# A latent-attention stack on one core: the second stage issues the same calls in another order

## What is computed

```python
x = x + _L0_xattn_ref(_layernorm(x, axis=-1), ctx_512, ...)
x = x + _L0_attn_ref(_layernorm(x, axis=-1), ...)
x = x + _L0_ffn_ref(_layernorm(x, axis=-1), ...)
x = x + _L1_xattn_ref(_layernorm(x, axis=-1), ctx_512, ...)
x = x + _L1_attn_ref(_layernorm(x, axis=-1), ...)
x = x + _L1_ffn_ref(_layernorm(x, axis=-1), ...)
```

## Time and profile before

| | us |
|---|---|
| median of three runs (1688.26 to 1689.56) | 1689.56 |
| the profiled execution, its own time | 1687.6 |
| its span in the profile | 1685.8 |
| the stage, first `score_x` to last `keep_hT` | 199.2 to 541.2 |

### The profile page before, as it was taken

One profiled execution on the slowest core, in us unless ns is written; L12 is line 12 of the kernel. 1 busy time (PEld: TensorE's weight loads), 2 busy tenths in 40 slices (PEclk: granted clock), 3 DMA queues, 4 the chain that ended last, 5 costly groups with the idle time before them and its releaser, 6 DMA issues. The chain is left out here.

```text
span 1685.8 us, 34006 instructions
## 1 busy us (share of the span) xinstructions
PE 1557.3 (92%) x14224; PEld 1087.3 (64%) x14224; DVE 1128.5 (67%) x1745; ACT 595.8 (35%) x1038; POOL 553.1 (33%) x885
## 2 busy tenths in 40 slices
PE   7999679989996588999999999999999996999999
PEld 3444357867783356777777777777777774565556
DVE  4665487588564667888877888878888833644433
ACT  2223134335332344444544444444444431111110
POOL 1200052123111344664554664554654431000000
PEclk9999779999996889999999999999999997999999
DMA  7533300010000012211212211212211113200000
GB/s 214 158 92 93 69 1 1 14 38 2 1 1 0 23 27 48 55 45 34 55 33 55 54 43 35 48 41 55 48 49 37 41 28 116 116 1 0 13 1 13
DMA packets 150536, 75.76 MB, mean 45 GB/s; under 512 B 128304, under 2 KB 131632, under 8 KB 148592
## 3 DMA queue, kind: packets, MB, share of 16 engines
q1 hardware_dynamic: 150384, 73.60, 17.1%
HBM read 55.73 MB, written 17.83 MB: 44 GB/s over the span
## 5 line engine op out<-in xcount | busy, mean ns | idle before, releaser
L1719 DVE SCALAR_TENSOR_TENSOR acc<-PS,wc,acc 128x504 f32<-128x504 f32 (+2 forms) x384 | 281.4, 733 | 93.2 <-ACT acc L1452 84.1
L2004 PE MATMUL PS<-HT,wgu 128*128 128x512 f32 x384 | 173.9, 598 | 0.6 <-ACT HT L2050 0.6
L1452 ACT ACTIVATE acc<-PS,wc 128x512 f32<-128x512 f32 x128 | 87.7, 685 | 171.8 <-PE PS L1183 120.0
L1183 PE MATMUL PS<-HT,wv 128*128 128x512 f32 x256 | 128.6, 626 | 11.4 <-DVE acc L1719 11.4
L1183 PE MATMUL PS<-HT,wkq 128*128 128x512 f32 x256 | 124.4, 610 | 6.6 <-DVE acc L1719 4.7
L1729 DVE SCALAR_TENSOR_TENSOR y<-th,acc 128x512 f32<-128x512 f32 x128 | 114.6, 895 | 22.7 <-ACT th L1456 21.5
L1642 POOL TENSOR_TENSOR rr<-nm,con 128x16 f32<-128x16 f32 x16 | 46.8, 2925 | 239.3 <-DVE nm L1747 239.3
L1200 PE MATMUL PS<-wz,HT 128*128 128x256 f32 x512 | 123.5, 389 | 0.8 <-DMA wz<-in_gdn_w 0.8
L2004 PEld LDWEIGHTS PS<-HT,wgu 128*128 128x128 f32 x384 | 73.3, 192 | 74.9 <-issue 72.8
L1346 PE MATMUL PS<-wo,ogT 128*128 128x256 f32 x512 | 115.3, 383 | 3.5 <-DVE dl L1782 2.4
L2140 DVE SCALAR_TENSOR_TENSOR act<-th,PS 128x512 f32<-128x512 f32 x48 | 33.0, 687 | 127.4 <-ACT th L2064 127.4
(11 more groups left out here) (252 smaller groups left out, 3045.6 us busy)
## 6 DMA issues: line engine op xcount, KB each, us to landing
a_rows<-AT SPq DMA_DIRECT2D x16, 512.0 KB, 2.6
wk<-in_l0x_k SPq DMA_DIRECT2D x16, 384.0 KB, 3.6
wgu<-in_moe_gu SPq DMA_DIRECT2D x6, 1024.0 KB, 14.9
queries_scratch<-tts SPq DMA_DIRECT2D x32, 128.0 KB, 2.7
wkq<-in_gdn_w SPq DMA_DIRECT2D x16, 256.0 KB, 2.7
wv<-in_gdn_w SPq DMA_DIRECT2D x16, 256.0 KB, 2.8
wz<-in_gdn_w SPq DMA_DIRECT2D x16, 256.0 KB, 3.3
wo<-in_gdn_w SPq DMA_DIRECT2D x16, 256.0 KB, 2.9
```

The source lines that it names most:

```text
L1183: mm = pe.matmul(PS[:, QB[q], :], w[:, o:o + DK], HT[:, k, f * 512:(f + 1) * 512], start=(k == 0), stop=(k == DC - 1))
L1452: a.activation(acc[:, f, :], PS[:, QB[q], :], ACT.Copy, scale=wc[:, h % 2, 4 * c + 3:4 * c + 4]).then_inc(s["tap"], 1)
L1719: v.scalar_tensor_tensor(a0, p0, wc[:, h % 2, 4 * c + 2 - k:4 * c + 3 - k], a0, ALU.mult, ALU.add).then_inc(s["conv"], 1)
L2004: mm = pe.matmul(PS[:, 2 * (i % 2) + w, :], wgu[:, m, k, w, :], HT[:, k, f * N:(f + 1) * N], start=(k == 0), stop=(k == DC - 1))
```

## The change

The lists of calls of all five engines in `phase2` are written in another order. No function, buffer, semaphore or wait changes, and each list has the same calls as before. SP loads tile 1 ahead of tile 0. Cut to the parts that the text speaks of:

```diff
-                load(0); load(1); load(2); load(3); load(4); load(5); load(6); load(7)
+                load(1); load(0); load(2); load(3); load(4); load(5); load(6); load(7)
...
-                score_x(0, 0); fold_down(); score_x(0, 1); score_x(1, 0); score_x(2, 0); turn_x(0, 0); score_x(3, 0)
-                turn_x(0, 1); context(0); score_x(1, 1); out_x(0); score_x(2, 1); turn_x(1, 0); turn_x(1, 1); turn(0, 0)
-                context(1); project(0, 0); out_x(1); turn_x(2, 0); scores(0, 0); turn_x(2, 1); score_x(3, 1); turn(1, 0)
...
-                down(7); turn(4, 3); turn_p(5, 1); scores(6, 1); values(5, 1); turn(7, 2); project_out(5, 1); project(7, 1)
-                turn(5, 3); turn_p(6, 1); scores(7, 1); values(6, 1); project_out(6, 1); turn(6, 3); turn_p(7, 1)
-                values(7, 1); project_out(7, 1); turn(7, 3)
+                score_x(1, 0); score_x(0, 0); fold_down(); score_x(0, 1); score_x(1, 1); score_x(2, 0); score_x(3, 0)
+                turn_x(0, 0); turn_x(0, 1); context(0); turn_x(1, 0); out_x(0); score_x(2, 1); turn_x(1, 1); score_x(3, 1)
+                context(1); turn_x(2, 0); out_x(1); turn(0, 0); turn_x(2, 1); project(0, 0); context(2); turn(1, 0)
+                turn_x(3, 0); scores(0, 0); project(1, 0); turn_x(3, 1); out_x(2); context(3); scores(1, 0); turn_p(0, 0)
...
+                down(6); project(5, 1); up_gate(7, 1); scores(5, 1); turn_p(4, 1); turn(6, 2); down(7); project(6, 1)
+                values(4, 1); turn(7, 2); project_out(4, 1); scores(6, 1); turn_p(5, 1); project(7, 1); values(5, 1)
+                turn(4, 3); scores(7, 1); project_out(5, 1); turn_p(6, 1); values(6, 1); project_out(6, 1); turn(5, 3)
+                turn_p(7, 1); turn(6, 3); values(7, 1); project_out(7, 1); turn(7, 3)
...
-                exp_x(0, 0); keep_fold(); exp_x(0, 1); keep_x(0, 0); keep_x(0, 1); exp_x(1, 0); keep_context(0); exp_x(2, 0)
-                exp_x(1, 1); keep_x(1, 0); exp_x(2, 1); keep_x(1, 1); keep_hT(0, 0); exp_x(3, 0); keep_context(1)
+                exp_x(1, 0); exp_x(0, 0); keep_fold(); exp_x(0, 1); keep_x(0, 0); keep_x(0, 1); exp_x(1, 1); keep_context(0)
+                keep_x(1, 0); exp_x(2, 0); exp_x(3, 0); keep_x(1, 1); exp_x(2, 1); keep_context(1); keep_x(2, 0)
...
-                share_x(0, 0); share_x(0, 1); scale_down(0); share_x(1, 0); scale_down(1); share_x(1, 1); root(0, 0)
+                share_x(1, 0); share_x(0, 0); share_x(0, 1); scale_down(0); share_x(1, 1); scale_down(1); share_x(2, 0)
...
-                spread_x(0, 0); sums_x(0, 0); spread_x(0, 1); butterfly(0); sums_x(0, 1); butterfly(1); spread_x(1, 0)
-                butterfly(2); sums_x(1, 0); spread_x(2, 0); spread_x(1, 1); residual(0, 0); spread_x(2, 1); sums_x(1, 1)
...
-                spread_x(4, 0); sums(2, 1); residual(1, 3); key_blocks(3, 1); stats(1, 3); spread_x(4, 1); apply(1, 3)
-                mask_spread(3, 1); sums_x(4, 0); residual(2, 3); sums(3, 1); stats(2, 3); sums_x(4, 1); spread_x(5, 0)
...
+                spread_x(1, 0); spread_x(0, 0); sums_x(1, 0); sums_x(0, 0); spread_x(0, 1); butterfly(0); sums_x(0, 1)
+                butterfly(1); spread_x(1, 1); butterfly(2); sums_x(1, 1); spread_x(2, 0); residual(0, 0); spread_x(3, 0)
...
+                apply(3, 2); residual(1, 3); stats(1, 3); spread_x(4, 0); apply(1, 3); key_blocks(3, 1); spread_x(4, 1)
+                mask_spread(3, 1); residual(2, 3); spread_x(5, 0); stats(2, 3); sums(3, 1); apply(2, 3); sums_x(4, 0)
...
+                mask_spread(6, 1); apply(4, 3); key_blocks(7, 1); sums(6, 1); mask_spread(7, 1); residual(5, 3)
```

More of the change, by code:

```diff
@@ L701, in _ @@
[L701 to L715, removed]
@@ new lines, in _ @@
+                turn_x(3, 0); scores(0, 0); project(1, 0); turn_x(3, 1); out_x(2); context(3); scores(1, 0); turn_p(0, 0)
+                turn(2, 0); out_x(3); values(0, 0); project(2, 0); project_out(0, 0); turn(3, 0); turn_p(1, 0); project(3, 0)
+                scores(2, 0); turn(0, 1); values(1, 0); hadamard(0); project_out(1, 0); up_gate(0, 0); scores(3, 0)
+                turn(1, 1); hadamard(1); turn_p(2, 0); up_gate(1, 0); values(2, 0); up_gate(0, 1); project_out(2, 0)
+                up_gate(1, 1); down(0); turn(2, 1); down(1); hadamard(2); turn(0, 2); turn_p(3, 0); up_gate(2, 0)
@@ new lines, in _ @@
+                values(3, 0); project(0, 1); project_out(3, 0); up_gate(2, 1); turn(1, 2); scores(0, 1); turn(3, 1)
+                project(1, 1); hadamard(3); down(2); up_gate(3, 0); scores(1, 1); turn(2, 2); turn_p(0, 1); project(2, 1)
+                up_gate(3, 1); values(0, 1); scores(2, 1); project_out(0, 1); down(3); turn_p(1, 1); values(1, 1); turn(0, 3)
+                project_out(1, 1); score_x(4, 0); turn(3, 2); project(3, 1); turn_p(2, 1); turn(1, 3); score_x(4, 1)
+                score_x(5, 0); scores(3, 1); values(2, 1); project_out(2, 1); score_x(5, 1); turn(2, 3); score_x(6, 0)
@@ new lines, in _ @@
+                turn_p(3, 1); turn_x(4, 0); values(3, 1); turn_x(4, 1); project_out(3, 1); score_x(6, 1); context(4)
+                turn_x(5, 0); out_x(4); turn_x(5, 1); turn(3, 3); turn_x(6, 0); score_x(7, 0); context(5); turn(4, 0)
+                turn_x(6, 1); out_x(5); score_x(7, 1); project(4, 0); context(6); turn(5, 0); turn_x(7, 0); scores(4, 0)
+                project(5, 0); turn_x(7, 1); out_x(6); context(7); scores(5, 0); turn_p(4, 0); out_x(7); turn(6, 0)
+                values(4, 0); project(6, 0); project_out(4, 0); turn(7, 0); turn_p(5, 0); project(7, 0); scores(6, 0)
@@ new lines, in _ @@
+                turn(4, 1); values(5, 0); hadamard(4); project_out(5, 0); up_gate(4, 0); scores(7, 0); turn(5, 1)
+                hadamard(5); turn_p(6, 0); up_gate(4, 1); values(6, 0); up_gate(5, 0); project_out(6, 0); turn_p(7, 0)
+                down(4); values(7, 0); turn(6, 1); up_gate(5, 1); hadamard(6); project_out(7, 0); up_gate(6, 0); down(5)
+                turn(4, 2); turn(7, 1); up_gate(6, 1); hadamard(7); project(4, 1); up_gate(7, 0); scores(4, 1); turn(5, 2)
+                down(6); project(5, 1); up_gate(7, 1); scores(5, 1); turn_p(4, 1); turn(6, 2); down(7); project(6, 1)
@@ L805, in _ @@
[L805 to L809, removed]
@@ L820, in _ @@
+                keep_hT(5, 3); keep_p(7, 1); keep_hT(6, 3); keep_o(7, 1); keep_hT(7, 3)
             @block.gpsimd
@@ new lines, in _ @@
+                spread_x(7, 0); sums_x(7, 0); residual(5, 0); stats(5, 0); spread_x(7, 1); apply(5, 0); key_blocks(4, 0)
+                sums_x(7, 1); mask_spread(4, 0); key_blocks(5, 0); sums(4, 0); residual(6, 0); stats(6, 0); apply(6, 0)
+                mask_spread(5, 0); residual(7, 0); stats(7, 0); sums(5, 0); apply(7, 0); residual(4, 1); stats(4, 1)
+                key_blocks(6, 0); apply(4, 1); mask_spread(6, 0); residual(5, 1); key_blocks(7, 0); stats(5, 1); sums(6, 0)
+                apply(5, 1); glu(4, 0); mask_spread(7, 0); sums(7, 0); glu(4, 1); glu(5, 0); residual(6, 1); stats(6, 1)
```

97 lines of the change are left out of this document (45 added, 52 removed).

## The result

| | before | changed | changed, a second time |
|---|---|---|---|
| median, us | 1688.91 (1687.77 to 1689.56) | 1671.19 (1666.14 to 1672.91) | 1671.74 (1669.61 to 1672.93) |
| ratio to before, 95% interval | | 0.9888 (0.9871 to 0.9906) | 0.9877 (0.9862 to 0.9892) |
| span in the profile | 1685.8 | 1664.3 | 1671.1 |
| first `score_x` to last `keep_hT` | 342.0 | 320.6 | 319.5 |
| behind the stage | 1144.6 | 1144.9 | 1152.2 |

The account below looks back on a forecast made before the run. PE was taken to bound four dense stretches, DVE the passage, waits both ends. Terms 6.0 - 0.6 + 2.0 - 1.8 + 2.4 + 2.0 - 0.4 + 4.6 = 14.2, less 1.8: 12.4 off 1689.56 gives 1677.2 us; range 1670 to 1686.

Parts of the forecast that it names:

- the whole plan holds: Rival: no loss at handovers, port free, end gives 6, passage up to its upper bound; 1670.3 to 1673.4 us, chance 0.17.
- self attentions: From `scores(0, 0)` to the first `up_gate`: PE's idle time falls from 2.5 to 0.5 us, so 2.0 won.
- feed-forward and passage: From `up_gate(0, 0)` to `scores(4, 0)`: 1.8 us lost in the feed-forward stretch, 2.4 won in the passage.
- The deduction of 1.8: Taken off the summed gain for some six short waits at handovers that the walk cannot see, 0.3 us each.
- The walk: New lists followed: full-clock trace durations, 0.1 us between engines; PE's progress compared at seven cuts, total gain 14.2 us.
- The end: Last calls of the stage: `scores(7, 1)` comes earlier, DVE's 4.63 us wait before the last masking goes; 4.6 us won.
- The start: Up to `scores(0, 0)`: PE's 4.90 us wait before `turn_x(1, 1)` goes and five calls get done earlier; 6.0 us won.
- The port: In the start, `apply(0, 0)` on DVE is held up by `share_x(3, 0)` on POOL through a shared port; 0.6 us lost.
- Passage: Passage to tiles 4 to 7: DVE's idle time shrinks despite PE's new 4.9 us wait for `spread_x(5, 0)`; 2.4 us won.
- Second half: Tiles 4 to 7 before the end: 2.0 us won in the self attentions, 0.4 lost in the feed-forward stretch.
- DVE takes the middle back: Rival: DVE-bound passage spends PE's lead from the start, only the second half counts; gain 6.2 us, 1683.4, chance 0.22.
- The clock stays low: Rival: PE stays at 1.2 GHz after the passage's new wait, making the kernel slower, 1697 with twenty such us; chance 0.06.

Follow-up runs that it names:

- nested kernels: Changed kernel's lists up to `turn_p(1, 1)`, `scores(4, 0)` or `down(7)`, remaining calls in the old order: ratios to before 0.9955, 0.9947, 0.9933.
- scores7_late: Changed kernel with `scores(7, 1)` moved behind `turn_p(6, 1)` on PE, as before: ratio to before 0.9931, stage 328.4 us.
- start_new: Kernel before with the new order only for the calls up to `turn_p(2, 0)`: ratio to before 1.0005, stage 339.6 us.
- passage_new: Kernel before with the new order only for the calls of the passage to tiles 4 to 7: ratio to before 1.0021, stage 342.0 us.
- fill_wait: Changed kernel with `spread_x(5, 0)` ahead of `mask_spread(3, 1)` on DVE: ratio to before 0.9895, stage 319.6 us.
- new_to_345: Changed kernel's lists up to `turn_p(1, 1)`, 345 us, remaining calls in the old order: ratio to before 0.9955, stage 331.3 us.

## Why the prediction was right in kind and short in size

The first median, 1671.19, lies below the forecast of 1674 to 1680, among the outcomes that had 0.17 under "the whole plan holds".

**What bounds the stage** held: the two ends are chains of waits and gave the two largest terms of the gain, DVE bounds the passage, and the dense stretches stayed dense (4.4 us idle in 198.7, 7.4 in 212.4 before).

**The terms, laid beside the profile.** The lead below is how much sooner PE begins a call, seen from the stage's start, plus PE's time for calls that it has done by then and had not before, less that for calls put off. That time is the prediction's own at `scores(0, 0)` (5.3), `scores(4, 0)` (5.4) and `down(7)` (-3.6), and -0.9 for one `turn_p` at the two `up_gate`. It is good to about 1 us.

| up to | term | forecast | measured, two profiles | lead |
|---|---|---|---|---|
| `scores(0, 0)` | start and port | 5.4 | 6.7, 6.4 | 6.7, 6.4 |
| `up_gate(0, 0)` | self attentions | 2.0 | 2.8, 2.7 | 9.5, 9.1 |
| `scores(4, 0)` | feed-forward and passage | 0.6 | 1.5, 1.5 | 11.0, 10.6 |
| `up_gate(4, 0)` | self attentions, 4 to 7 | 2.0 | 2.9, 2.9 | 13.9, 13.5 |
| `down(7)` | feed-forward, 4 to 7 | -0.4 | 1.1, 1.1 | 15.0, 14.6 |
| the end | end | 4.6 | 6.4, 7.9 | 21.4, 22.5 |
| | sum | 14.2 | 21.4, 22.5 | |

**The deduction of 1.8** for tight handovers is the step that failed most plainly: it had the wrong sign. Every term came out above its forecast before anything was taken off, together by 7.2 to 8.3 us. With the 1.8 the stage was forecast 9.0 to 10.1 short.

**The walk** had the order of events right and its steps too slow: `scores(0, 0)` at 249.4 came at 248.22 (0.5 of it an earlier start of the whole stage), `scores(4, 0)` at 402 came at 398.83. It took durations "in the trace at full clock", and rows of PE that follow each other overlap: the 20 calls of the changed kernel from `scores(0, 0)` up to `up_gate(0, 0)` last 30.1 us one by one and take 28.4 together. How much of the shortfall this makes isn't shown, since the prediction already used some distances from start to start.

**The end**, 4.6 for 6.4 to 7.9, is the term with the largest miss. I had priced the wait of 4.63 alone and put the clock at nothing. From `down(7)` to the end of the stage:

| | length | PE busy (matmuls) | clock |
|---|---|---|---|
| before | 37.3 | 22.8 (205) | 0.70 |
| changed | 34.5 | 23.6 (255) | 0.88 |
| changed, a second time | 32.9 | 22.0 (255) | 1.00 |

The profile shows 50 matmuls more there in about the same busy time. Before, `turn_p(6, 1)` and `scores(7, 1)` lost 1.8 to the half clock ahead of the last masking; now both run at full. The 9.4 to 10.5 of the nested kernels are more than this term: their last step also holds what the old end loses of the second half. In `scores7_late`, `project_out(6, 1)` waits 4.21 for ACT, which it doesn't before (0.52): ACT's new list has `exp(7, 1)` ahead of `keep_o(6, 1)`, which it needs. `turn_p(7, 1)` behind it waits for POOL all the same, so this wait isn't what makes that kernel slow.

**The start.** That the wait of 4.90 would go was right, but by itself it is worth 1 to 2; the rest is the lists of the engines keeping in step, which `start_new` lacks behind its cut. Up to 2.4 us of the measured term can be chance, since the old start took 48.5 to 50.9 in three profiles. *The port*, 0.6: `apply(0, 0)` took 0.89 for 0.41, so 0.48. As before it ended 0.15 after the first of the two `share_x`, and didn't wait for the second. The Trainium skill, SBUF — State Buffer, section "Who interferes with whom", has the two lock each other out for a whole instruction; the trace agrees for one instruction.

**Passage**, 2.4 forecast: +0.1 in the nested kernels, and a loss in `passage_new`. The wait was forecast to 0.1 (4.9 for 4.82), and `fill_wait` shows that it costs nothing in the changed kernel. **Second half**, 1.6 forecast: 1.4 in the nested kernels agrees by luck, since the lead at `down(7)` rose by 4.0.

**The rivals.** "DVE takes the middle back" fell: the new order of the passage gives nothing, but the first lead isn't spent there. In `new_to_345` `scores(4, 0)` comes 10.6 us sooner than before, with the same calls done, and the stage is 10.7 shorter. "The whole plan holds" is the one that came closest in its number, and two of its reasons held: no loss at the handovers, and an end of 6 (6.4 to 7.9). The port cost nearly what was forecast, though, and the passage didn't reach its upper bound; the rest came from terms that it left alone. "The clock stays low" fell: 0.88 in the passage, 1.00 behind it. At half clock run not only `score_x(5, 1)` but `score_x(6, 0)`, `turn_p(3, 1)` and most of `turn_x(4, 0)` behind it. The Trainium skill, TensorE: Matmul & The Clock Gate, section "HAM oscillation", warns of waits that bring the lower clock back each time; here the passage agrees, in every profile of it, and where DVE is the bound `fill_wait` shows no cost of the call that it brings back to full clock.

**What is left open.** 21.4 of the stage stand against 17.7 of the medians, in code that is the same; the changes of the total are on average 2 us above those of the stage. Whether that is the stretch behind it, or a long stage in the one profile of the kernel before, isn't shown.

**What was to show it**: no wait before `turn_x(1, 1)`, PE idle for 8.9 up to `scores(0, 0)` (forecast 9), clock 0.84, the new wait of 4.8, no wait of L927 in the end, all as said. The last `keep_hT` was to start near 528 and starts at 519.00.

## What to carry to other kernels

Where every engine has its order written out, price a new order by what the engines gain together: a lead of the one that is the bound lasts only as far as the lists of those that feed it keep up, and a part of such a change, tried alone, may show little of what it is worth in the whole. A step between two nested kernels also measures what stands behind the cut; lay the call times of the two profiles side by side before giving it to a term. When walking a list by hand, sum the distances from start to start that the trace shows, not the durations, and take nothing off for caution unless a row shows the loss. Price the clock beside the waits: half of this gain was busy time. Before filling a wait, look which engine is busy meanwhile: if that one is the bound, the wait moves to the next call.

## What the runs showed of the hardware that was not expected

The unchanged code behind the stage took 1144.6 to 1152.2 us from one profile to the next, and two profiles of the same kernel differ by 7.3 there and by 1.2 in the stage. And the same calls behind the same waits ran at either clock. `turn_p(7, 1)` waited 1.07 before and ran in 1.97 us; in the changed kernel it waited 1.32 and ran in 1.09. From `down(7)` on the granted clock was 0.88 in one profile of the changed kernel and 1.00 in the other. In `scores7_late`, a wait of 1.73 with two calls at half clock behind it (1.97 and 1.99 us for 1.09 each, at 505.10) took 3.5 us of PE's time just where PE was waited for.
